# Two residual conv blocks on one core: the projections' image-pair loop written out on all engines, SyncE's side transfers spread between the stores of chunks

## The reference, cut to what matters

```python
x = x + L0(_gn(x), w, b)             # shifted 8x8 window mixing, 16 heads
x = x + L1(_gn(x), w_qkv, w_dw, w_pw, w_proj, bn_gamma, bn_beta, bn_mean, bn_var)

def L1(x, ...):
    qkv = einsum('bchw,oc->bohw', x, w_qkv)          # the projections: 256 -> 768 channels
    y = conv5x5_depthwise(qkv, w_dw)                 # the taps
    y = conv1x1_grouped(y, w_pw)                     # 96 groups of 8
    mqkv = concatenate([qkv, y], axis=1)             # 64 heads of q, k, v
    vk = einsum('bhdn,bhen->bhde', pad1(v), relu(k))
    out = einsum('bhde,bhen->bhdn', vk, relu(q))
    out = out[:, :, :-1] / (out[:, :, -1:] + 1e-15)
    out = einsum('bchw,oc->bohw', out, w_proj)
    return out * inv + (bn_beta - bn_mean * inv)     # inv = bn_gamma / sqrt(bn_var + 1e-5)
```

## Time and profile before

| | us |
|---|---|
| median of 3 runs | 2471.97 |
| the profiled execution | 2473.01 |
| its span, first to last instruction of the program | 2471.3 |
| the projections in it: barrier to barrier | about 262 to 1007 |
| TensorE (PE) busy | 2355.5 |
| VectorE (DVE), ScalarE (ACT), GpSimd (POOL) busy | 1994.8, 1494.2, 1098.4 |

### The profile page before, as it was taken

The page is one execution under the profiler, slowest core; times in us unless marked ns, Lnnn a source line. Parts: engine busy times, 40 slices in busy tenths (PEclk is TensorE's granted clock), DMA queues, the critical chain, the costliest instruction groups (busy, mean ns, idle before and its releaser), DMA issues. The chain is left out here.

```text
span 2471.3 us, 66794 instructions
## 1 busy us (share of the span) xinstructions
PE 2355.5 (95%) x25485; PEld 1880.1 (76%) x25485; DVE 1994.8 (81%) x2653; ACT 1494.2 (60%) x1864; POOL 1098.4 (44%) x1476
## 2 busy tenths in 40 slices
PE   5999799999999999799999999999999899999998
PEld 5889688877787888578888888888888656666666
DVE  7887588788788877788888888888888688888785
ACT  5787566666565666566676666676767434433442
POOL 6722387787787788200000000000000068888887
PEclk9999899999999999899999999999999999999999
DMA  7874689989889989988888888888888767777774
GB/s 279 337 304 177 203 292 339 334 284 331 305 278 331 335 295 310 264 204 205 211 209 207 208 211 209 209 206 210 209 208 210 234 242 279 278 273 272 272 273 136
DMA packets 300973, 628.38 MB, mean 254 GB/s; under 512 B 50784, under 2 KB 252256, under 8 KB 291552
## 3 DMA queue, kind: packets, MB, share of 16 engines
q1 hardware_dynamic: 295072, 590.38, 77.4%
q10 hardware_dynamic: 4688, 31.63, 3.6%
q0 software_dynamic: 1008, 3.67, 0.4%
HBM read 327.81 MB, written 300.94 MB: 254 GB/s over the span
## 5 line engine op out<-in xcount | busy, mean ns | idle before, releaser
L1570 PE MATMUL c_ps<-dh,wh 128*128 128x512 f32 x1152 | 462.5, 401 | 15.4 <-DVE wl L1725 10.3
L1485 ACT ACTIVATE dh<-image 128x1632 fp32r<-128x1632 f32 x192 | 301.7, 1571 | 266.4 <-PE c_ps L1570 251.1
L1570 PE MATMUL c_ps<-dh,wl 128*128 128x512 f32 x1152 | 454.4, 394 | 0.0
L1570 PE MATMUL c_ps<-dl,wh 128*128 128x512 f32 x1152 | 452.9, 393 | 0.7 <-issue 0.7
L1934 POOL TENSOR_TENSOR ql<-image,qh 128x1024 fp32r<-128x1024 f32 x1 | 2.4, 2356 | 962.1 <-DVE ql L2165 962.1
L1678 DVE TENSOR_TENSOR dl<-image,dh 128x1632 fp32r<-128x1632 f32 x192 | 356.4, 1856 | 73.6 <-ACT dh L1485 73.5
L1132 PE MATMUL o_ps<-xh,wqh 128*128 128x512 f32 x768 | 318.7, 415 | 11.3 <-issue 8.0
L1922 POOL TENSOR_TENSOR ql<-image,qh 128x1024 fp32r<-128x1024 f32 x126 | 301.5, 2425 | 9.0 <-ACT qh L1953 9.0
L1132 PE MATMUL o_ps<-xl,wqh 128*128 128x512 f32 x768 | 303.0, 394 | 0.0
L1132 PE MATMUL o_ps<-xh,wql 128*128 128x512 f32 x768 | 301.7, 393 | 0.0
L1570 PEld LDWEIGHTS c_ps<-dh,wh 128*128 128x128 f32 x1152 | 216.8, 188 | 67.6 <-DVE wl L1725 10.4
(11 more groups left out here) (212 smaller groups left out, 5113.5 us busy)
## 6 DMA issues: line engine op xcount, KB each, us to landing
qkv_scratch<-stage SPq DMA_DIRECT2D x384, 408.0 KB, 4.4
image<-qkv_scratch SPq DMA_DIRECT2D x189, 816.0 KB, 6.3
yq_scratch<-qy SPq DMA_DIRECT2D x64, 512.0 KB, 6.7
image<-qr_scratch SPq DMA_DIRECT2D x128, 256.0 KB, 6.1
image<-yq_scratch SPq DMA_DIRECT2D x128, 256.0 KB, 5.2
ox<-x_scratch SPq DMA_DIRECT2D x8, 4096.0 KB, 14.8
qr_scratch<-qs SPq DMA_DIRECT2D x126, 256.0 KB, 3.5
out<-ox SPq DMA_DIRECT2D x7, 4096.0 KB, 12.7
```

The costliest lines, as they stand in the source:

```text
L1485: act.activation(by_image(dh[kind]), as_loaded(kind), ACT.Copy).then_inc(hi_ready, 1)
L1570: last = pe.matmul(c_ps[:, m, :], w[hp][:, kind, part, o:o + P], d[kind][:, n0:n0 + IMG * HALF * NB], start=(k == 0), stop=(k == 5))
```

## The change

The projections' five engine functions call a new helper that emits all four pairs one after the other, so image numbers are constants everywhere: no jump, no register arithmetic, no second wait of `Own`. `over_image_pairs` stays for `output`. And the 26 side transfers become a generator from which SyncE takes one step per chunk, between `queries(n - 1)` and `keys_values(n, 1)`: the 16 sorts in the 16 chunks of images 0 and 1, the 6 loads of pointwise weights in chunks 0 to 5 of image 2, and the 4 vectors together in chunk 6 of image 2.

```diff
+def over_image_pairs_unrolled(body):
+
+    for i in range(B // 2):
+        body(i, i == B // 2 - 1)
...
-            for t in range(QT):
-                rows = w_pw.rearrange("(h k o) c y x -> k h o (c y x)", k=3, o=D)[t // 2, HT * (t % 2):HT * (t % 2) + HT, :, :]
-                sp.dma_start(K["pw_raw"][:, t, :], rows).then_inc(K["pw_loaded"], 16)
...
-            sp.wait_ge(K["taps_out"], 16 * QT)
-            for p in range(NPH):
-                src = taps_dram.rearrange("t (h c) p n -> p c (t h) n", c=D)[p, :, :, :]
-                sp.dma_start(sorted_dram[D * p:D * p + D, :, :], src).then_inc(K["taps_sorted"], 16)
+            def aside():
+
+                for p in range(NPH):
+                    if p == 0:
+                        sp.wait_ge(K["taps_out"], 16 * QT)
+                    src = taps_dram.rearrange("t (h c) p n -> p c (t h) n", c=D)[p, :, :, :]
+                    sp.dma_start(sorted_dram[D * p:D * p + D, :, :], src).then_inc(K["taps_sorted"], 16)
+                    yield
+                for t in range(QT):
+                    rows = w_pw.rearrange("(h k o) c y x -> k h o (c y x)", k=3, o=D)[t // 2, HT * (t % 2):HT * (t % 2) + HT, :, :]
+                    sp.dma_start(K["pw_raw"][:, t, :], rows).then_inc(K["pw_loaded"], 16)
+                    yield
+                with nc.allow_non_contiguous_dma(reason="256 values each"):
+                    for n, v in bn_in.items():
+                        sp.dma_start(K["bn"][n][:, :], v.rearrange("(t p) -> p t", p=P)).then_inc(K["bn_loaded"], 16)
+                yield
+
+            loads_aside = aside()
...
                         if n > 0:
                             queries(n - 1)
+                        next(loads_aside, None)
                         keys_values(n, 1)
                     queries(NCH - 1)
-            over_image_pairs(sp, body)
+            over_image_pairs_unrolled(body)
```

More of the change, by code:

```diff
@@ L819, in _ @@
         def _(sp):
-            for t in range(QT):
-                rows = w_pw.rearrange("(h k o) c y x -> k h o (c y x)", k=3, o=D)[t // 2, HT * (t % 2):HT * (t % 2) + HT, :, :]
-                sp.dma_start(K["pw_raw"][:, t, :], rows).then_inc(K["pw_loaded"], 16)
-            with nc.allow_non_contiguous_dma(reason="256 values each"):
-                for n, v in bn_in.items():
-                    sp.dma_start(K["bn"][n][:, :], v.rearrange("(t p) -> p t", p=P)).then_inc(K["bn_loaded"], 16)
-            sp.wait_ge(K["taps_out"], 16 * QT)
-            for p in range(NPH):
-                src = taps_dram.rearrange("t (h c) p n -> p c (t h) n", c=D)[p, :, :, :]
-                sp.dma_start(sorted_dram[D * p:D * p + D, :, :], src).then_inc(K["taps_sorted"], 16)
+            def aside():
[14 more added lines that the diff above has]
+            loads_aside = aside()
             for par in range(2):
@@ L949, in body @@
                     queries(NCH - 1, last_body and par == 1)
-            over_image_pairs(pool, body)
+            over_image_pairs_unrolled(body)
         @block.scalar
@@ L1095, in body @@
                         load_half(b, par, 0)
-            over_image_pairs(act, body)
+            over_image_pairs_unrolled(body)
         @block.tensor
@@ L1196, in body @@
                             sum_vk(b, n, u)
-            over_image_pairs(pe, body)
+            over_image_pairs_unrolled(body)
         @block.vector
@@ L1333, in body @@
                                       AX.X, ALU.add)
-            over_image_pairs(dve, body)
+            over_image_pairs_unrolled(body)
 def over_head_pairs(eng, body):
```

## The result

The changed kernel takes **2459.84 us**, the median of 4 runs (2451.32 to 2461.94), beside 2472.88 us of the kernel before (4 runs, 2470.35 to 2477.15). That is 13.0 us less by the medians; the ratio is 0.9942 with a 95% interval from 0.993 to 0.9953, 14.3 us less by it, faster by more than 0.2%. The forecast was 2455, the range 2450 to 2465. The profiled execution is the shortest of the four, 2451.32 us (span 2449.6), 8.5 us under the median.

The account below looks back on a forecast made before the run. TensorE, busy 2355.5 of 2471.3 us, was the bound, leaving its idle or half-clock time in the projections. 2473.0 - 5.7 - 13.5 + 0.8 + 1.3 = 2455.9 us, 2455 in medians; range 2450 to 2465.

Parts of the forecast that it names:

- Image 0: the stores start late: Projections, image 0: side transfers delay the first stores, so TensorE waits 4.78 us; moving them gains 5.7 us.
- The loop written out: Projections, images 2 to 5: at 88.8 us each, 13.5 us less, with 0.8 us kept back for image 5.
- The body of the loop: Projections, images 2 to 5: register instructions before waits cost 1.4 us per image, 5.6 us in all.
- The turn: one jump: Between images 3 and 4: TensorE's 3.95 us jump back, with half clock behind it, makes image 4 6.3 us longer.
- The 16 sorts: One per chunk in images 0 and 1: image 0's eight cost nothing, image 1's wait grows; +1.3 us.
- a chunk's stores landing: Image 0: sorts hide between stores landing, 4.4 us after issue, and the buffer's next use two 11 us chunks later.
- The prediction's own sign of being wrong: Waits of `pt_ps` for `kv` over 2 us at the start of images 1 to 5 would mean DMA binds.
- the sorts hurt wherever they are: Rival, 5%: each sort holds TensorE by its 1.33 us issue, 21.3 us come back; 2475 us, no change.
- The 10 small loads: Image 2, chunks 0 to 6: hidden behind the same cover, cost nothing; 3.6 us once if the cover were gone.
- no new cost at all: Lower bound of the sum: both gains in full and no added cost from sorts or waits, 2453 us.
- DMA binds the faster pace: Rival, 12%: full DMA engines make images 1 to 5 wait 1.7 us each, sorts cost 2.5; 2463 us.
- Another loop loses its place: Rival, 3%: moved code makes the convolution's 14 turns stall at TensorE's jump, costing 85 us; 2540 us.

Follow-up runs that it names:

- these two runs: Kernel before with only TensorE's loop written out, 2469.91 us; changed kernel with TensorE alone kept in its loop, 2467.77 us.
- the earlier placement: Changed kernel with the 16 sorts in chunks 0 to 5 of image 0 (3, 3, 3, 3, 2, 2): 2456.26 us, ratio 0.9935.
- the repeat: The changed kernel run again, unedited: 2460.1 us, ratio 0.9955.
- The cut-off kernel: Changed kernel ended behind the projections, convolution and output left out: 1012.65 us, beside 1025.62 us for the kernel before cut the same way.
- the kernel with the side transfers alone: Kernel before with loops kept, 16 sorts one per chunk in images 0 and 1, small loads in image 6: 2469.59 us, ratio 0.9987.

## Why the prediction held, and where it was off

- **Image 0: the stores start late** was right. Chunks 1 to 7 went from 83.5 to 77.3 us, a gain of 6.2 where 5.7 was the term, and wait and lower clock are gone. But as a gain of the kernel it hardly exists: with the sorts' cost set against it, the moved transfers bring 2.4 us alone and about 1 us beside the written-out loop (2461.14 against 2459.84 and 2460.1).
- **The loop written out** was right in its sum: 368.7 - 355.0 = 13.7 us in the trace, against 13.5 - 0.8 = 12.7, and 12 us where this part was run alone. **The body of the loop** was right too, in the traces: TensorE's part alone brought images 2 and 3 from 90.2 to 88.8 us.
- **"The turn: one jump"** was incomplete. The sum was not hurt, since the change writes out all engines; that part is luck. The step named TensorE's jump as the cause, and TensorE's loop alone written out left image 4 at 96.6 us. Every engine stalls behind its own jump, 5.7 to 6.4 us in these two runs; in the trace of before TensorE's hid those of the others, because the view of the waits shows what came last.
- **The 16 sorts** are the term of the sum that was mis-sized: +1.3 us, with the eight in image 0 at nothing. Moving them into the mixing takes the changed kernel from 2459.8 and 2460.1 us to 2452.8, and with the small loads back in their place to 2453.5, so with the places that the change gives them they cost 6 to 7 us in the medians, **about 7 us**, and 4 to 9 us by the ratios. The step took a sort's price from the DMA time it moves, 0.84 us. What the traces showed in its place is that, beside an image's load, the issue behind a sort holds SyncE for up to 7.7 us, that the stage's buffer comes late by it, and that TensorE then waits 2 to 3 us, in two of the five traces with such waits followed by a stretch at a lower clock (not in the change's own). And the cover in image 0, "a chunk's stores landing", wasn't enough: all 16 in image 0 still cost 3 to 6 us by the medians, though for the earlier placement the intervals overlap with those of the kernels without sorts there. The prediction's own sign of being wrong, a wait for `kv` over 2 us in the loads' stretch of images 1 to 5, stood in image 1 with 2.42 us. The rival "the sorts hurt wherever they are", 21.3 us, fell: in the mixing they cost nothing that can be seen, and in the change a third of that.
- **The 10 small loads** cost nothing that can be told, as said.
- **The bound "no new cost at all"**, 2453 us, is what the kernels without that cost take: 2452.8 and 2453.5. That closes the sum: 2453 + 7 = 2460. The forecast's own range, 2450 to 2460, just held the first median, 2459.84, and missed the repeat's 2460.1. The range to 2465 held because the rival "DMA binds the faster pace", 2463, had pulled its end up, and that is luck in part: the cause of that rival, full DMA engines in images with a load, is the one that acted, but waits over 1 us came only where sorts were: images 3 to 6 are at 88.3 to 88.9 us in both traces of the change.
- **Another loop loses its place** fell: the convolution's 14 jumps take 0.24 us at most from their new place. The Trainium skill (*Runtime: NRT & Kernel Launch*, Instruction fetch mechanics) has two statements here, and its TensorE memory of 2048 instructions is again the one that agrees with this row and with the 6.37 us of the jump over two images; the window of 512 agrees with the latter only.

**What stays open.** The traced runs of the changed kernel, 2451.3 and 2453.6 us, are 6 to 11 us shorter than its plain ones. The cut-off kernel puts the missing gain into the projections, and its trace shows one longer form, by 4.6 us in images 1 and 2. In both kernels with the sorts in the mixing the traced run, 2452.8 and 2452.9 us, lies amid the plain ones. That points to the sorts, but no plain run can be looked into; and against it, the kernel with TensorE's loop alone written out, with no sort among its stores, has its traced run as the shortest of eleven too (2466.42, median 2469.91). Why a traced one of the change escapes wasn't found. Of the 7 us the change's own trace shows about half: its images 1 and 2 are 2.4 and 1.3 us longer than 88.2, and the rest is seen in medians alone. As wholes the traced runs of the change (2451.3, 2453.6) and of the kernels without these sorts (2452.8, 2452.9) don't differ: behind the start of image 6 the change's trace is 3.0 us shorter than that with the sorts in the mixing, which no edit explains. Nor is it settled why some of these kernels spread over 9 us and others over 3, or what makes an issue take up to 7.7 us behind a sort: the rows show that it does, with the DMA engines full, and no more. Whether the sorts' short rows matter, or only that they are transfers, no run tells.

## What to carry to other kernels

Price a transfer that is moved between others not by the bytes it moves but by how long it holds its queue where it now stands: where the window shows DMA engines full, the issue behind it can take fifteen times the median (7.69 us against 0.5 here), and a buffer two steps on comes late. Look for the stretch whose DMA share is low and put it there (0.3 to 0.45 here); "hidden" in an image that runs at 0.9 may mean deferred to the next. When a change has two parts, run each alone: here one of them brought about 1 us. And where a loop's jump back stalls, write it out on all engines: TensorE alone left in it was enough to keep the stall.

## What the hardware showed that was not expected

- An issue of a store of `stage` took SyncE 7.69 us at most in the change, with a sort now and then between stores beside a load (8.67 in the kernel with the side transfers alone), 2.58 us (sorts in the mixing) and 3.64 us (the kernel before) without, 0.4 to 0.5 us in the median; the sort's own issue took 0.66 us there, but 6.91 us where two stood together:

```profile
L833 SPq DMA_DIRECT2D tap_sorted<-tap_scratch x16: 659/774/6912, 275.7 to 360.4; - x16
```

- The jump back over two images stalled TensorE for 3.95 us in one kernel and 6.37 us in the other, both in its jump's own length. On the other four engines 5.7 to 6.4 us pass from the jump to the next instruction of the loop, while the jump itself shows 0.05 to 0.06 us. On those engines the jumps' lengths alone show nothing; the time to the first instruction behind them does.
- A wait of 2 to 3 us was sometimes enough for the granted clock to fall: 0.66 and 0.72 in the 5 us windows behind waits of 3.03 and 2.00 us, 0.58 in 4 us behind one of 2.07, but 1.00 in 6 us behind one of 2.42. So such a wait can cost more than its own length, and its length alone doesn't tell.
